# First attention stage of an audio tower: the key copy put first on VectorE, feature products before token products, query transposes in another PSUM bank, maxima negated in the reduction

## The reference, cut to what matters

```python
h = layer_norm(x, norm1_g, norm1_b)
q = h @ Wq.T
kv = h @ Wkv.T                       # keys and values are the same tensor
q, k, v = split_heads(q), split_heads(kv), split_heads(kv)      # 8 heads of 8 channels
# head 0: local attention in windows
dots = einsum('bnie,bnje->bnij', bq * d ** -0.5, bk)
out = einsum('bnij,bnje->bnie', softmax(dots), bv)
# heads 1 to 7: linear attention
qs = softmax(q, axis=-1) * d ** -0.5
ks = softmax(k, axis=-2)             # over the tokens
ctx = einsum('bhnd,bhne->bhde', ks, v)
out = einsum('bhnd,bhde->bhne', qs, ctx)
y = concatenate(heads) @ Wproj.T + bproj
x = x + y
```

## Time and profile before

| | us |
|---|---|
| median of 3 runs | 1123.39 (1122.95 to 1123.62) |
| the profiled execution, its own time | 1124.06 |
| its span (first to last instruction) | 1121.9 |
| first attention stage, from its first transpose to its last statistics | 202.57 to 325.12 |
| PE busy over the whole span | 987.0 (88%) |
| DVE, ACT, POOL busy | 698.7 (62%), 663.6 (59%), 516.3 (46%) |

### The profile page before, as it was taken

The page is one execution under the profiler, slowest core; times in us unless marked ns, Lnnn a source line. Parts: engine busy times, 40 slices in busy tenths (PEclk is TensorE's granted clock), DMA queues, the critical chain, the costliest instruction groups (busy, mean ns, idle before and its releaser), DMA issues.

```text
span 1121.9 us, 34992 instructions
## 1 busy us (share of the span) xinstructions
PE 987.0 (88%) x12202; PEld 677.4 (60%) x12202; DVE 698.7 (62%) x1954; ACT 663.6 (59%) x1224; POOL 516.3 (46%) x812
## 2 busy tenths in 40 slices
PE   3789876688869799999999998699999999949998
PEld 0245444466647587777777777266666666635555
DVE  3356652577747556766667675288888888844443
ACT  1134543477755567676767673377777777635554
POOL 0001101577747367676767765245555555441110
PEclk9989996599989899999999998599999999979999
DMA  8432100000000000000000000000000000000001
GB/s 243 74 58 38 19 1 1 1 1 0 0 1 1 1 3 3 1 0 0 0 0 0 0 2 2 1 2 3 0 0 0 0 0 0 1 1 15 19 19 25
DMA packets 10769, 14.99 MB, mean 13 GB/s; under 512 B 9296, under 2 KB 9296, under 8 KB 9680
## 3 DMA queue, kind: packets, MB, share of 16 engines
q1 hardware_dynamic: 10704, 14.13, 5.9%
HBM read 12.03 MB, written 2.10 MB: 13 GB/s over the span
## 4 chain that ended last, share of the span: by engine, by line
PE 53%; issue 11%; POOL 7%; DVE 7%; ACT 2%; POOLq 1%; DVEq 0%; ACTq 0%
PE ps L1758 6%; PE ps L1331 5%; PE ps L1343 5%; POOL e_acc L1273 5%; PE ps L1780 4%; PE ps L1766 4%; PE ps L1748 3%; PE ps L1922 3%; PE ps L1746 3%; PE ps L1955 3%; DVE a_rmax L1804 2%; DVE a_diff L1807 2%; PE ps L1105 1%; PE ps L608 1%; PE ps L789 1%
## 5 line engine op out<-in xcount | busy, mean ns | idle before, releaser
L1540 ACT ACTIVATE e_hid<-ps,cst 128x512 f32<-128x512 f32 x256 | 161.6, 682 | 78.4 <-PE ps L1331 78.4
L1343 PEld LDWEIGHTS ps<-ew,e_hid 128*64 128x64 f32 x4096 | 130.0, 138 | 42.4 <-issue 29.1
L1273 POOL TENSOR_TENSOR e_acc<-e_acc,e_part 128x512 f32<-128x512 f32 x96 | 123.6, 1288 | 64.8 <-DVE e_part L1478 64.6
L1478 DVE TENSOR_TENSOR e_part<-ps,e_wt 128x512 f32<-128x512 f32 x128 | 88.4, 691 | 99.1 <-PE ps L1343 77.0
L1343 PE MATMUL ps<-ew,e_hid 128*64 128x64 f32 x4096 | 147.6, 225 | 0.0
L1331 PE MATMUL ps<-e_xs,ew 64*128 64x256 f32 x1024 | 146.7, 406 | 0.0
L1804 DVE TENSOR_REDUCE a_rmax<-ps 128x8 f32<-128x1024 f32 x64 | 78.2, 1222 | 38.2 <-PE ps L1758 37.1
L1331 PEld LDWEIGHTS ps<-e_xs,ew 64*128 64x128 f32 x1024 | 89.3, 188 | 16.0 <-issue 2.5
L1713 POOL TENSOR_TENSOR a_sum<-a_part 128x256 f32<-128x256 f32 x64 | 46.5, 727 | 108.1 <-DVE a_part L1815 108.1
L204 POOL TENSOR_TENSOR t_prob<-t_ex,t_rscale 128x512 f32<-128x512 f32 x8 | 12.0, 1502 | 172.2 <-DVE t_rscale L377 172.2
L1766 PEld LDWEIGHTS ps<-cst,a_ex 128*128 128x128 f32 x512 | 55.6, 141 | 50.6 <-issue 41.5
(11 more groups left out here) (260 smaller groups left out, 2035.7 us busy)
## 6 DMA issues: line engine op xcount, KB each, us to landing
x_in<-x_dram SPq DMA_DIRECT2D x48, 128.0 KB, 4.7
cst<-cst_dram SPq DMA_DIRECT2D x1, 3037.0 KB, 16.9
out_dram<-e_res SPq DMA_DIRECT2D x16, 128.0 KB, 1.9
ew<-ew_dram SPq DMA_DIRECT2D x1, 1024.0 KB, 18.9
cst<-cst_dram SPq DMA_DIRECT2D x1, 704.0 KB, 7.4
ew<-ew_dram SPq DMA_DIRECT2D x1, 512.0 KB, 20.4
cst<-cst_dram SPq DMA_DIRECT2D x1, 329.5 KB, 3.1
```

The costliest lines, as they stand in the source:

```text
L1273: eng.tensor_tensor(acc[:, :, :, :], acc[:, :, :, :], part[n % RING][:, :, :, :], ALU.add).then_inc(sum_sb.sem, 1)
L1343: mm = eng.matmul(m.ps[rows, 6 + n % 2, to:to + C], hid[e % 4][:, a:a + C], w2[:, e * C:e * C + C], start=True, stop=True)
L1478: eng.tensor_tensor(part[n % RING][:, :, :, :], m.ps[:, 6 + n % 2, :].rearrange("p (s j c) -> p s j c", s=TS, j=2), wt[b][:, :, 2 * n:2 * ...
L1540: nc.scalar.activation(hid[e % 4][:, :].rearrange("p (r t) -> p r t", r=2), m.ps[:, 2 + 2 * (n % 2):4 + 2 * (n % 2), j * 256:(j + 1) * 256 ...
```

## The change

It touches `attention0` alone.

1. **Maxima.** `kmax` with `kneg`, and `lmax` with `lneg`, become one reduction each that writes the negated maximum. SCALE, which the second instruction carried for the local scores and which ACT's exponential applied, is folded into the weights and the bias of the queries' features once, ahead of the loop.
2. **Query transposes** go to the lower half of bank 1, where the features of the keys stood, and no longer to bank 0. `turn_queries` now waits for the feature copies of group g (a round old) instead of for the newest `xs`; `turn` loses its wait, and `features` gets one, for the copy `qsT` of the group before the last.
3. **PE** issues the feature products ahead of the token products.
4. **DVE** issues `keys` (the copy `ek`) first in the round; `query_maxima` stands behind `key_maxima` and `local_sums`; the four statistics are split in two and two.

```diff
@@ pe
         def turn(g, b):
             eng.wait_ge(norm_sb.sem, norm_sb.at(g))
-            eng.wait_ge(q_sb.sem, q_sb.at(g - 3))
             eng.wait_ge(xs_sb.sem, xs_sb.at(g - 1))
...
         def features(g, b):
             eng.wait_ge(xs_sb.sem, xs_sb.at(g))
             eng.wait_ge(kv_sb.sem, kv_sb.at(g - 1))
             eng.wait_ge(q0_sb.sem, q0_sb.at(g - 1))
+            eng.wait_ge(q_sb.sem, q_sb.at(g - 2))
...
         def turn_queries(g, newest):
             eng.wait_ge(q_soft.sem, q_soft.at(g))
-            eng.wait_ge(xs_sb.sem, xs_sb.at(newest))
+            eng.wait_ge(kv_sb.sem, kv_sb.at(newest))
+            eng.wait_ge(q0_sb.sem, q0_sb.at(newest))
             settle(eng, m)
             for p in range(NP):
-                mm = eng.transpose(m.ps[:, 0, HT + p * P:HT + (p + 1) * P],
+                mm = eng.transpose(m.ps[:, 1, p * P:(p + 1) * P],
...
-                turn_queries(g - 1, g + 1 if left else TG - 1)
+                turn_queries(g - 1, g if left is not None else TG - 1)
                 turn_probabilities(g - 1)
                 context(g - 1, 1 - b)
             if left:
+                features(g + 1, 1 - b)
                 tokens(g + 1, 1 - b)
-                features(g + 1, 1 - b)
@@ dve
         def key_maxima(g):
             eng.wait_ge(kv_sb.sem, kv_sb.at(g))
-            eng.tensor_reduce(kmax[:, :], kvT[:, :].rearrange("p (n t) -> p n t", n=NP), AX,
-                              ALU.max).then_inc(k_neg.sem, 1)
-            eng.wait_ge(k_neg.sem, k_neg.at(g, 1))
             eng.wait_ge(k_exp.sem, k_exp.at(g - 1))
-            eng.tensor_scalar(kneg[:, :], kmax[:, :], -1.0, None, ALU.mult).then_inc(k_neg.sem, 1)
+            eng.tensor_reduce(kneg[:, :], kvT[:, :].rearrange("p (n t) -> p n t", n=NP), AX,
+                              ALU.max, negate=True).then_inc(k_neg.sem, 1)
 
         def local_maxima(g):
             eng.wait_ge(local_ps.sem, local_ps.at(g))
-            eng.tensor_reduce(lmax[:, :, :], m.ps[:, 4:6, 0:HT].rearrange("p r (n t) -> p r n t", n=NP), AX,
-                              ALU.max).then_inc(local_neg.sem, 1)
-            eng.wait_ge(local_neg.sem, local_neg.at(g, 1))
             eng.wait_ge(local_exp.sem, local_exp.at(g - 1))
-            eng.tensor_scalar(lneg[:, :, :], lmax[:, :, :], -SCALE, None, ALU.mult).then_inc(local_neg.sem, 1)
+            eng.tensor_reduce(lneg[:, :, :], m.ps[:, 4:6, 0:HT].rearrange("p r (n t) -> p r n t", n=NP), AX,
+                              ALU.max, negate=True).then_inc(local_neg.sem, 1)
...
         def rest(g, b, left, back):
+            old = not isinstance(g, int) or g >= 2
+            if back:
+                keys(g - 1)
             if left is not None:
                 local_maxima(g)
                 key_sums(g)
-            if back:
-                keys(g - 1)
-            if left is not None:
                 query_sums(g)
             if back:
                 context(g - 1)
+            if old:
+                count(g - 2, 0)
             if left:
                 tokens(g + 1, 1 - b)
-                query_maxima(g + 1, 1 - b)
-            if not isinstance(g, int) or g >= 2:
-                count(g - 2)
-            if left:
                 key_maxima(g + 1)
             if left is not None:
                 local_sums(g)
+            if left:
+                query_maxima(g + 1, 1 - b)
+            if old:
+                count(g - 2, 1)
             if back:
                 out(g - 1)
@@ act
         def local(g):
                     nc.scalar.activation(lex[:, r, p, :], m.ps[:, 4 + r, p * P:(p + 1) * P], ACT.Exp,
-                                         bias=lneg[:, r, p:p + 1], scale=SCALE,
+                                         bias=lneg[:, r, p:p + 1],
...
-            nc.scalar.activation(qsT[:, :], m.ps[:, 0, HT:NT], ACT.Identity).then_inc(q_sb.sem, 1)
+            nc.scalar.activation(qsT[:, :], m.ps[:, 1, 0:HT], ACT.Identity).then_inc(q_sb.sem, 1)
```

More of the change, by code:

```diff
@@ L640, in attention0 @@
     bias_kv, bias_q, bias_tok = sb("bias_kv", [P, 1]), sb("bias_q", [P, 1]), sb("bias_tok", [P, P])
-    lmax, lneg, lsum, lrec = (sb(n, [P, 2, NP]) for n in ("lmax", "lneg", "lsum", "lrec"))
-    kmax, kneg, ksum, krec = (sb(n, [P, NP]) for n in ("kmax", "kneg", "ksum", "krec"))
+    lneg, lsum, lrec = (sb(n, [P, 2, NP]) for n in ("lneg", "lsum", "lrec"))
+    kneg, ksum, krec = (sb(n, [P, NP]) for n in ("kneg", "ksum", "krec"))
     qmax, qsum, qrec = (sb(n, [P, TS * HEADS]) for n in ("qmax", "qsum", "qrec"))
@@ L657, in attention0 @@
     kv_sb, q0_sb, tok_sb = step("kv_sb"), step("q0_sb"), step("tok_sb")
-    local_ps, local_neg, local_exp = step("local_ps"), step("local_neg", 2), step("local_exp", TS)
+    local_ps, local_neg, local_exp = step("local_ps"), step("local_neg"), step("local_exp", TS)
     local_rec, local_prob = step("local_rec"), step("local_prob")
-    k_neg, k_exp, k_rec = step("k_neg", 2), step("k_exp", NP), step("k_rec")
+    k_neg, k_exp, k_rec = step("k_neg"), step("k_exp", NP), step("k_rec")
     q_max, q_diff, q_exp, q_rec, q_soft = step("q_max"), step("q_diff"), step("q_exp"), step("q_rec", 2), step("q_soft")
@@ L950, in out, with count @@
                               ALU.add).then_inc(x1_sb.sem, 1)
-        def count(g):
+        def count(g, half):
             eng.wait_ge(x1_sb.sem, x1_sb.at(g))
-            stats(eng, m, m.y, g, TS, x1_stat.sem)
+            stats(eng, m, m.y, g, TS, x1_stat.sem, (TS // 2 * half, TS // 2 * (half + 1)))
         def rest(g, b, left, back):
+            old = not isinstance(g, int) or g >= 2
+            if back:
+                keys(g - 1)
             if left is not None:
@@ L978, in dve @@
         eng.wait_ge(m.cst2_sem, 16)
-        for w, name in ((w_kv, "wkv2"), (w_q, "wq2"), (w_tok, "wtok")):
-            eng.tensor_scalar(w[:, :], col(m, name), col(m, "n1g"), None, ALU.mult).then_inc(m.a0_scaled, 1)
+        for w, name, scale in ((w_kv, "wkv2", 1.0), (w_q, "wq2", SCALE), (w_tok, "wtok", 1.0)):
+            eng.tensor_scalar(w[:, :], col(m, name), col(m, "n1g"), scale, ALU.mult, ALU.mult).then_inc(m.a0_scaled, 1)
         eng.wait_ge(pre, 3)
         eng.tensor_copy(bias_kv[:, :], m.ps[:, 0, 0:1]).then_inc(pre_sb, 1)
-        eng.tensor_copy(bias_q[:, :], m.ps[:, 1, 0:1]).then_inc(pre_sb, 1)
+        eng.tensor_scalar(bias_q[:, :], m.ps[:, 1, 0:1], SCALE, None, ALU.mult).then_inc(pre_sb, 1)
         eng.tensor_copy(bias_tok[:, :], m.ps[:, 6, 0:P]).then_inc(pre_sb, 1)
@@ L989, in dve @@
         lagged(eng, TG, lambda g, b: None, rest)
-        count(TG - 1)
+        count(TG - 1, 0)
+        count(TG - 1, 1)
     def act(eng):
```

## The result

| | before | changed | ratio, 95% interval |
|---|---|---|---|
| first comparison, 4 runs each | 1123.17 us (1120.87 to 1123.62) | 1105.92 (1102.13 to 1107.32) | 0.9845 (0.9815 to 0.9875) |
| the same two kernels again, 20 and 6 runs | 1117.53 (1112.92 to 1123.59) | 1105.76 (1102.69 to 1108.07) | 0.988 (0.9855 to 0.9906) |

The account below looks back on a forecast made before the run. A chain of waits through `ek`, 6.98 us a round, was taken to bound the attention. Twelve rounds falling to 6.3 give 8.2, plus 0.2 at both ends: 8.4 off 1123.39, so 1115.0, range 1111.5 to 1119.5.

Parts of the forecast that it names:

- `ek` first: DVE: `ek` starts behind the add to `y`, not 1.34 us behind the maxima's start, removing the old chain's largest piece.
- the bank: PE: query transposes in bank 1 wait for copies a round old instead of the newest `xs`, at no cost.
- the place of the new wait: PE's probability transposes newly wait for POOL's `lprob`; the path leading back to `lprob` bounds the round.
- The sum of the new loop: From probability transposes over PE, DVE and POOL back: 6.40 by durations, less DVE overlaps of 0.05 to 0.2; 6.3 taken.
- Features first: PE to ACT: features come about 0.65 us earlier, only partly usable; token products come 1.08 us later.
- Negated maxima: DVE: `kneg` leaves the new chain; writing the negative costs between 0 and 0.17 us, taken as nothing.
- Head and tail: Ends of the attention: head gives 0.2 us or nothing, tail 0.1; 0.2 for both in the sum.
- What lies outside the stage: Rest of the kernel: no change counted; the 8.4 us gain applied to the median of 1123.39 gives 1115.0.
- A: New chain cheaper than its rows; ACT's chain or POOL decides at 5.7 to 6.1; 1111.4 at 6.0; chance 0.12.
- B: Rounds of 6.6 to 6.8 us: reduction inherits `kneg`'s wait, handoffs cost more or POOL late; 1119.8 at 6.7; chance 0.22.
- C: Attention rounds: no difference, as `turn_probabilities` waits as long as `ek` did; 1122 to 1124 us; chance 0.05.
- D: Head: PE's wait for `lprob` delays the clock's rise, some 2.5 us per half-clock round; 1127.5 with five; chance 0.03.

Follow-up runs that it names:

- key copy first alone: Kernel before with only the key copy `ek` moved ahead of DVE's local maxima: 1111.58 us, ratio 0.9933, 6.44 a round.
- key copy behind: Changed kernel with `ek` put back behind the local maxima on DVE: 1111.03 us, ratio 0.9927 to before, 6.30 a round.
- `qmax` early: Changed kernel with the query maxima put back directly behind the token copy, ahead of the key maxima: 1101.54 us, ratio 0.9845 to before.
- pairs put back: Changed kernel with each negated reduction again a reduction and a multiplication by -1: 1112.72 us, ratio 0.9937 to before.
- bank alone: Kernel before with only the query transposes moved to bank 1 with their new waits: 1117.94 us, ratio 1.0001, 6.96 a round.
- `lprob` first: Changed kernel with `lprob` ahead of `values` and `qd` on POOL: 1101.45 us; with `lrec` also ahead of the token copy: 1099.27 and 1103.67.

## Why the prediction was wrong, point by point

- **`ek` first, the bank, the place of the new wait: right.** The context no longer waits for `ek`, the query transposes wait for nothing, and the new loop runs over exactly the instructions that were listed.
- **The sum of the new loop: right in its path, mis-sized. This is the first step that failed.** 6.40 by durations, 6.3 forecast, 6.03 measured. Of the 0.27 between the last two, 0.11 is the token copy: 0.72 forecast, 0.61 measured. The 0.72 came from a row in which `qmax` follows and waits for the copy's own result; in the new order `kneg` follows, which does not. Another 0.10 is the three instructions behind it, two reductions and `lrec`: 1.00 forecast, 0.32+0.09+0.39 = 0.80 measured, which is the 0.2 at the end of the allowance of 0.05 to 0.2, where the forecast took 0.1. None of the three waits for the result of the one ahead of it, and each starts 0.08 to 0.09 before that one's end. The last 0.06 is PE: transposes and context 0.94 for 1.05, features and tokens 1.78 for 1.73. The 12 rounds gave 11.2 us (83.59 against 72.40) where 8.2 were forecast.
- **Features first**: forecast as a part of 0.65; it gives 0.08.
- **Negated maxima**: right, the reductions were not stretched (0.407 to 0.420 and 0.679 to 0.692). The sum has neither multiplication on the new loop, so it does not suffer; but I took only `kneg` for a cost in the rounds. `lneg` stood in the queue ahead of the token copy.
- **Head and tail: the second step that failed.** 0.2 for both ends went into the sum; they gave 1.2. Counted from L516, round 1's transposes stood at 21.1 before and 20.5 after, so the head to there gave 0.6, to round 2's 0.5. From round 14 on another 0.8 came, 0.2 in round 15 and 0.6 in round 16. No single edit is its cause: key copy first alone has 0.6 of it, but so has the changed kernel with the key copy behind.
- **What lies outside the stage: taken as unchanged, from a base of 1123.39. This is the third step that failed.** The forecast of 8.4 against 12.4 is the error of the mechanism's sizes: 3.0 in the rounds, 1.0 at the ends. By itself it would have given 1111.0, just below the range. The other 5 us between 12.4 and 17.3 lie outside the stage, and by the experiments they are scatter, of which three runs of 1122.95 to 1123.62 had shown nothing: 56 more span 1112.3 to 1124.1.
- **The rivals.** A named the length, 5.7 to 6.1, but not its cause: neither ACT's chain nor POOL alone decides, as `qmax` early shows with 5.85. B, C and D did not occur. For B, even with the pairs put back a round is 6.47, below its 6.6. Its 0.48 is the longest `kneg` of 0.65 less the 0.17 of a small instruction; no run shows a reduction that inherits that wait. That gaps on PE put off the rise of the clock, as D has it, was my guess from the earlier trace rows, and no run shows it. For D, the rise of the clock lies about 23.9 behind L516 in both kernels, by my estimate from PEclk in stretches of 2 us (0.76 from 216 to 218 in the changed kernel, 0.97 from 220 to 222 before).
- **The range and the chances.** The range was said to take most of A. By A's own price of 1111.4 at 6.0 it left out all but the rounds from just above 6.0 to 6.1. The chances of what is faster add up to at most 0.90, not 0.91.

Open remains what in the head lets the clock rise early in one kernel and late in another, and what sets the scatter of 3 to 5 us outside the attention. The MLP, the experts and the second attention together were 3.1 to 3.6 us shorter in both profiles of the changed kernel than in both of the kernel before; but key copy first alone has 50.1, 322.4 and 296.4, 3.1 shorter, and the bank alone 50.1, 323.4 and 294.2, 4.3 shorter, with an attention of 128.3. So it does not come from the change as such.

## What to carry to other kernels

When in-order engines hand work round in a loop, list the loop's instructions and add start-to-start distances, not durations, taken from a place where the same neighbours follow without a wait. Look at what stands ahead of the awaited instruction in its own queue before looking at what it costs: one line moved on DVE, alone, gave half of this gain (a round of 6.97 to 6.44), and one more on POOL in the changed kernel (`lprob` ahead of `qd`) brings the loop to where PE's queue has no gap (6.03 to 5.82). A few runs that agree do not show the scatter of a kernel; cut the profile at stage borders and compare the stage that was changed.

## What the runs showed of the hardware that I had not expected

- From the token copy to `qmax`, neighbouring DVE instructions of the changed kernel overlap by 0.08 to 0.09: 0.69 long and followed after 0.61, 0.41 after 0.32, 0.17 after 0.09. In the kernel before, where the second waits for the first one's result, the distance is longer than the duration: the key maxima take 0.40 and `kneg` follows after 0.43, and the same token copy of 0.69 is followed by `qmax` after 0.72.
- With the maxima in pairs, a multiplication of 4 elements per partition on DVE took 0.63 next to a POOL instruction (261.42), against 0.17 alone (299.92).
- The same head can run at either clock. Two profiles in the same five-microsecond stretches (us, busy us, PEclk, DMA share, GB/s), the changed kernel:

```profile
200.00:205.00 5.00, 3.51 (x14) 2.41 (x16) 1.53 (x3) 1.48 (x4) 3.01 (x6) 0.50 0.00 0
205.00:210.00 5.00, 4.53 (x22) 3.06 (x21) 1.53 (x4) 3.54 (x16) 2.25 (x5) 0.50 0.00 0
```

and the one with `qmax` early:

```profile
200.00:205.00 5.00, 3.50 (x15) 2.28 (x16) 1.53 (x3) 1.34 (x4) 3.01 (x6) 0.61 0.00 0
205.00:210.00 5.00, 3.83 (x34) 2.80 (x35) 3.06 (x8) 3.82 (x17) 2.97 (x7) 1.00 0.00 0
```

With the same busy time of PE until 205 (3.51 and 3.50), the second is at full clock (1.00) from 205 on, where the changed kernel rises only in the stretch from 215 to 220 (0.80). It reached round 1's transposes 18.2 after L516 instead of 20.5. The edit cannot have set off the rise: PE's first local scores start 11.64 behind L516 in both, and the clock had gone up by then (they take 0.72 there, 1.23 in the changed kernel). So a difference of 2 us in one head is by itself no evidence for an edit. The three profiles with `lprob` first have short heads too (18.8 to 19.6); how much of that is their edit was not separated from the clock.
